# VectorE's order in the attention stage set anew: keys, logits, division and second maximum; logits in another bank; one product left out

## What is computed

```
# cross attention: 16 heads of 8 features, 77 keys per sequence
q = (query @ Wq.T + bq).reshape(B, T, H, HD)      # query = layernorm(x)
k = (key_value @ Wk.T + bk) ...; v = (key_value @ Wv.T + bv) ...
attn = softmax(einsum('bhtd,bhnd->bhtn', q, k) * scale)
x = x + einsum('bhtn,bhnd->bhtd', attn, v) @ Wo.T + bo
# routing, on xf = layernorm(x)
logits = xf @ gate_w.T; probs = softmax(logits)
top_p, top_i = top_k(probs, 2); w = top_p / (sum(top_p) + 1e-09)
rank = cumsum(one_hot(top_i), axis=0) - 1         # place of a token in its expert's list
keep = rank < capacity                            # capacity = 1280
```

## Time and profile before

| | |
|---|---|
| time, median of 3 runs | 1022.3 us (1021.0 to 1023.09) |
| the profiled execution: time | 1019.92 us |
| its span, first to last instruction | 1017.9 us |
| mean granted clock of TensorE | 0.958 of full |
| busy: TensorE, weight loads | 896.1 us, 631.8 us |
| busy: VectorE, ScalarE, GpSimd | 589.0, 468.8, 515.3 us |
| largest groups on TensorE in the middle stage | scores (line 1223) 100.7 us, turned scores (1240) 86.1, weighing (1260) 69.7 |

### The profile page before, as it was taken

The page is one execution under the profiler, slowest core; times in us unless marked ns, Lnnn a source line. Parts: engine busy times, 40 slices in busy tenths (PEclk is TensorE's granted clock), DMA queues, the critical chain, the costliest instruction groups (busy, mean ns, idle before and its releaser), DMA issues.

```text
span 1017.9 us, 26993 instructions
## 1 busy us (share of the span) xinstructions
PE 896.1 (88%) x9394; PEld 631.8 (62%) x9394; DVE 589.0 (58%) x1890; ACT 468.8 (46%) x721; POOL 515.3 (51%) x715
## 2 busy tenths in 40 slices
PE   3699999999999999999999999998349999999960
PEld 1577777776666666666666666666226767667650
DVE  5677777777556676667666766765402222344436
ACT  1256566566445555455555555545123434334320
POOL 4334444454422255555555555555626666666670
PEclk9799999999999999999999999999669999999995
DMA  4369500000000000000000001000021333245408
GB/s 124 104 239 339 191 0 0 0 1 1 7 8 8 8 30 23 29 21 19 12 16 14 15 15 29 9 10 11 16 84 51 102 89 108 80 138 166 147 25 330
DMA packets 49912, 66.68 MB, mean 66 GB/s; under 512 B 12662, under 2 KB 27813, under 8 KB 49824
## 3 DMA queue, kind: packets, MB, share of 16 engines
q1 hardware_dynamic: 38448, 52.14, 15.9%
q0 software_dynamic: 9216, 8.42, 2.8%
q10 hardware_dynamic: 2160, 4.86, 1.2%
HBM read 33.83 MB, written 42.09 MB: 75 GB/s over the span
## 4 chain that ended last, share of the span: by engine, by line
PE 57%; DVE 9%; issue 6%; POOL 2%; DMA 2%; ACT 1%; DVEq 1%; POOLq 0%; SPq 0%; ACTq 0%
PE psum L1677 13%; PE psum L1223 7%; PE psum L1689 7%; PE psum L1260 5%; PE psum L1240 4%; DVE Kb L911 2%; PE psum L1671 2%; PE psum L1273 2%; PE psum L1282 2%; PE psum L1210 2%; DVE Y L1603 2%; PE psum L1226 1%; PE psum L1268 1%; PE psum L594 1%; PE psum L1294 1%
## 5 line engine op out<-in xcount | busy, mean ns | idle before, releaser
L1571 POOL DMA_INDIRECT expert_out<-yo,token x160 | 156.2, 976 | 89.2 <-issue 70.8
L1135 ACT ACTIVATE PT<-psum,key_bias 77x2048 f32<-77x2048 f32 x64 | 125.7, 1964 | 131.1 <-PE psum L1243 131.0
L819 POOL DMA_INDIRECT dispatched<-z,idx x128 | 129.0, 1008 | 84.8 <-issue 42.4
L1614 DVE TENSOR_TENSOR h<-psum,act_g 128x512 f32<-128x512 f32 x80 | 55.3, 692 | 150.7 <-PE psum L1677 150.7
L894 DVE TENSOR_REDUCE top_score<-psum 128x8 f32<-128x616 f32 x128 | 101.9, 796 | 62.1 <-PE psum L1226 60.1
L1223 PE MATMUL psum<-Kb,qT 32*128 32x308 f32 x512 | 100.7, 469 | 0.0
L1649 ACT ACTIVATE act_g<-psum 128x512 f32<-128x512 f32 x80 | 47.8, 597 | 89.2 <-PE psum L1677 89.2
L1240 PE MATMUL psum<-qT,Kb 32*77 32x128 f32 x2048 | 86.1, 283 | 0.0
L1689 PE MATMUL psum<-down,h 128*128 128x128 f32 x640 | 78.1, 275 | 0.8 <-DVE h L1614 0.8
L1677 PE MATMUL psum<-xT,gate 128*128 128x512 f32 (+1 forms) x192 | 77.1, 532 | 0.8 <-ACT xT L1634 0.8
L1689 PEld LDWEIGHTS psum<-down,h 128*128 128x128 f32 x640 | 74.7, 192 | 2.1 <-DVE h L1614 1.7
(11 more groups left out here) (163 smaller groups left out, 1726.6 us busy)
## 6 DMA issues: line engine op xcount, KB each, us to landing
dispatched<-zeros SPq DMA_DIRECT2D x40, 258.0 KB, 2.8
xin<-dispatched SPq DMA_DIRECT2D x40, 258.0 KB, 4.2
expert_out<-zeros SPq DMA_DIRECT2D x32, 256.0 KB, 2.0
X<-in_x SPq DMA_DIRECT2D x16, 256.0 KB, 2.7
yb<-expert_out SPq DMA_DIRECT2D x16, 256.0 KB, 4.0
Y<-expert_out SPq DMA_DIRECT2D x7, 512.0 KB, 8.1
out<-Y ACTq DMA_DIRECT2D x7, 512.0 KB, 6.7
expert_out<-yo,token POOLq DMA_INDIRECT x160, 2.2
```

The costliest lines, as they stand in the source:

```text
L819: pool.indirect_dma_start(xg, bass.IndirectOffsetOnAxis(ap=idx[par][:, t, k:k + 1], axis=0), z4[par][:, t, :], None, bounds_check=ROWS - 1 ...
L1135: nc.scalar.activation(PT[j % 2][:], T.rearrange("p a c -> p (a c)"), ACT.Exp, bias=key_bias[:, bass.ds(b, 1)]).then_inc(s["PT_ready"], 1)
L1571: pool.indirect_dma_start(yt[slot], bass.IndirectOffsetOnAxis(ap=token[i][:, t:t + 1], axis=0), yo[i][:, t, :], None, bounds_check=P * B - ...
```

## The change

- `logits_down` now reads `gate_ps` in bank 0, beside the scores' columns (320 on), instead of in `misc`. It waits for the second half of the scores of batch 4(g + 2) + 2, of the quarter that it stands in (S_ps), instead of for the keys' product. `gate` waits for the first maximum of that quarter (top_ready).
- VectorE, quarter 0: `keys_out` stands right after the first maximum, then `logits_down`, then `normalise`, then the second maximum. Before: logits, second maximum, keys, division.
- VectorE: `ln_stats` and `ln_moments` with n = 3 move from quarter 0 of group g - 2 to quarter 3 of group g - 3, on either side of the steps 13 and 14.
- VectorE: routing steps 3 to 5 move ahead of `add_out`, and steps 6 to 8 from quarter 2 to the end of quarter 1.
- TensorE: the product of `wq` and `z3T` ahead of the turn of `o` is gone, with the waits on `dl_ready`.
- The hardware loop covers groups 4 to 11 instead of 4 to 13; groups 12 and 13 are written out.

```diff
-        gate_ps = misc[:, 320:320 + G4 * E].rearrange("p (t e) -> p t e", t=G4)
+        gate_ps = banks[0][:, 320:320 + G4 * E].rearrange("p (t e) -> p t e", t=G4)
...
-            with eng.Fori(4, NG - 3, 2) as g:
+            with eng.Fori(4, NG - 5, 2) as g:
...
             def logits_down(g):
-                if group(g + 3):
-                    dve.wait_ge(s["k_ps"], g + 4)
+                if group(g + 2):
+                    dve.wait_ge(s["S_ps"], 4 * (G4 * (g + 2) + 2) + 4)
                 dve.wait_ge(s["gate_ps"], g + 1)
...
                     if j == 0:
-                        if group(g + 2):
-                            ln_stats(g + 2, 3, stat3, xrow)
+                        if isinstance(g, int) and g == 0:
+                            ln_stats(2, 3, stat3, xrow)
+                            ln_moments(2, 3, stat3, mom3)
                         if group(g + 1):
                             queries_out(g + 1, other)
...
                     if j == 0:
-                        if group(g + 2):
-                            ln_moments(g + 2, 3, stat3, mom3)
+                        if group(g + 1):
+                            keys_out(g + 1, other)
                         if group(g - 2):
                             logits_down(g - 2)
+                        if batch(b - 1):
+                            normalise(b - 1, G4 - 1, g - 1)
                     if j == 1:
-                        routed(0, 1, 2)
+                        routed(0, 1, 2, 3, 4, 5)
                         if group(g - 1):
                             add_out(g - 1)
                     if j == 2:
-                        routed(6, 7, 8, 9)
+                        routed(9)
                     if j == 3:
+                        if group(g + 3):
+                            ln_stats(g + 3, 3, stat3, xrow)
                         routed(13, 14)
+                        if group(g + 3):
+                            ln_moments(g + 3, 3, stat3, mom3)
 
                     if batch(b + 2):
                         tops(b + 2, j % 2, 1)
-                    if j == 0 and group(g + 1):
-                        keys_out(g + 1, other)
-                    if batch(b - 1):
-                        normalise(b - 1, (j - 1) % G4, g if j else g - 1)
+                    if j > 0 and batch(b - 1):
+                        normalise(b - 1, j - 1, g)
                     if j == 1:
-                        routed(3, 4, 5)
+                        routed(6, 7, 8)
...
             def turn_out(g):
-                nc.tensor.matmul(misc, wq[:], z3T[:], start=True, stop=True)
                 pe.wait_ge(s["o_ready"], G4 * g + G4)
...
             def gate(g):
                 pe.wait_ge(s["z4T_ready"], g + 1)
+                pe.wait_ge(s["top_ready"], 2 * (G4 * (g + 2) + 2) + 1 if group(g + 2) else 2 * NB)
...
                     if j == 1 and group(g - 1):
                         if group(g + 1):
                             pe.wait_ge(s["Kb_ready"], g + 2)
-                        if group(g - 2):
-                            pe.wait_ge(s["dl_ready"], 2 * g - 2)
                         turn_out(g - 1)
```

More of the change, by code:

```diff
@@ L735, in groups @@
                 steps(g, g % 2)
-            with eng.Fori(4, NG - 3, 2) as g:
+            with eng.Fori(4, NG - 5, 2) as g:
                 steps(g, 0)
                 steps(g + 1, 1)
-            for g in range(NG - 2, NG + 3):
+            for g in range(NG - 4, NG + 3):
                 steps(g, g % 2)
```

## The result

The changed kernel took 993.7 us (median; the kernel before 1022.7 us beside it, 1021.0 to 1026.9). The ratio of the two is 0.970, with a 95% interval of 0.966 to 0.974. The forecast was 992.5 us in a range of 986 to 1003. The profiled execution took 991.8 us, its span 990.0, 27.9 less than before. The medians in this document count every execution, the ratios only those within 1.5% of the kernel's fastest: that leaves out one of the four here, which took 1513.0 us at a mean granted clock of 0.61 and of which no trace was taken, so that its cause is open, and in the experiments one of the four with the division last and five of the ten of the unaltered changed kernel.

What follows compares the result with a forecast made beforehand. The prediction took TensorE's nearly unbroken chain of matmuls in the attention stage as the bound. Terms 9.1 + 14.8 + 2.0 + 4.8 + 0.4 - 1.3 = 29.8 us gave 990.1 profiled, 992.5 us as median, range 986 to 1003.

Steps and rivals of the forecast that it cites:

- The chain: Attention stage: TensorE's matmuls run almost without a break, so a microsecond leaving them leaves the kernel 13 or 14 times over.
- the rival in which ScalarE sets the pace: Attention loop: ScalarE paces it, so TensorE would wait elsewhere for what it saves; no change, 1020 to 1024 us; chance 0.04.
- 0.65 (keys): First quarter of a group: TensorE's wait for the keys before the overwritten product goes, 14 x 0.65 = 9.1 us.
- 0.96 (product): First quarter, before the output's turn: removing the overwritten product saves 0.96 us a group, 14.8 us in all.
- 0.37 (`hot`): Before the rank products: routing steps 3 to 8 come earlier, so TensorE's wait for `hot` goes, 13 x 0.37 = 4.8 us.
- 0.15 (qT, 2.0 in 13): First quarter: with statistics moved to the fourth, TensorE's wait for qT goes, 4 times 0.5, 2.0 us in all.
- the 1.3 us given back to ScalarE: ScalarE normalises for the router until 493.69, so exponentials start slightly later than they could: 0.1 x 13 = 1.3 us lost.
- The margins: Slack before TensorE waits: 0.4 us for the first quarter's second maximum, 0.5 for Mx in the first and fourth quarters.
- Both rivals with a late engine: VectorE late at the first quarter's turn, 999.5 us, chance 0.13; GpSimd late with Mx in the fourth, 999 us, chance 0.08.
- The tail: Last 16 scatters, before the experts: the whole shift reaches them, plus some 0.4 us; the last scatter starts near 716.
- The clock, as a rival: TensorE without the overwritten product: its granted clock falls and the kernel gets slower; chance 0.04 together with other causes.

## Why the prediction was right, point by point

- **The chain.** That TensorE's unbroken row of matmuls sets the pace was the ground of the sum, and it stood: of 30 waits none is left, the group went from 27.35 to 25.12 us, and the rival in which ScalarE sets the pace is refuted, since ScalarE's work did not change.
- **The sum.** A group was to lose 0.65 (keys), 0.96 (product), 0.37 (`hot`) and 0.15 (qT, 2.0 in 13), less 0.1. It lost 2.23. The experiments give the product 0.93 and `hot` 0.42; with 0.65 for the keys and 0.15 for qT, which no run singled out, that is 2.15, and 0.08 stay open. So the step on `hot` was sized a little low (0.37 for 0.42), and the 1.3 us given back to ScalarE, taken because it would still be normalising, were not given back: the exponentials follow without a gap, and TensorE never waits for them.
- **The margins.** The second maximum started 6.58 us after the query product against 6.7, and Mx in quarter 3 started at 485.52 and was done 0.8 us ahead of its turn, at 486.81 (0.5 forecast). Doubling the maximum brought waits of 0.25 us on average, so the margin was as thin as stated. Both rivals with a late engine were rightly placed as near and did not come, but for one wait for Mx of 0.45 us, in group 15, and one for the second maximum of 0.32 us, in group 0.
- **The tail and the experts: errors that cancel.** The last scatter was to start near 716 and started at 715.70 (745.96 before), 30.3 us earlier against 29.8 in the sum. The path there was another: at the turn of `o` in quarter 1 of group 15 (666.09 against 697.68) the shift was already 31.6, since each group lost more than counted, and the tail gave 1.3 back instead of adding 0.4. That the two nearly cancel is luck. The rows from group 15 on:

```profile
672.90 0.22 PE L1237 MATMUL psum<-ident_b,Mx 128*128 128x128 bf16 x1 [0.45 <-POOL Mx L795]
...
684.80 1.12 PE L1280 MATMUL psum<-ident,o 128*128 128x128 f32 x4 [0.68 <-DVE o L904]
...
715.70 0.97 POOL L820 DMA_INDIRECT dispatched<-z,idx  x1 [0.30 <-issue]
```

The last turn of `o` took 1.12 us (0.60 at the full clock), and the stretch before the experts ran at 0.72 and 0.54: the clock fell earlier, against the tail's work, than before. Then the span came out only 27.9 us shorter, so 2.4 of the 30.3 were lost in the experts' stage. The fall of the clock after the wait at 852.40, seen above, has 2.2 of them. The sum had no term for it. So the profiled execution took 991.8 us instead of the 990.1 of the sum, and the median lay 1.9 us above it instead of 2.4.
- **The clock, as a rival.** It was priced at "one group in four" and given 0.04 with other causes. In groups 2 to 14 of the changed kernel's profiled execution it did not come. The run with the maximum three times, and the kernel before without its product, show that the mechanism is real where a gap of 0.9 to 1.2 us stands in each group. In the changed kernel real matmuls fill the product's place, so there is no such gap. The Trainium skill, "TensorE: Matmul & The Clock Gate", section "Part 1: The HAM clock gate (the 'warmup' mystery)", says that the engine is throttled by default and that activity lifts it; the traces agree, since each fall named here follows idle time of TensorE. In these traces gaps well under a microsecond were enough for some of the falls (0.39 us once), and far longer ones than those did not always bring one (2.34 us at 882.51).
- **What was missed.** On a chip of the other kind the changed kernel is slower than before. Nothing in the trace of the kernel before, taken on a chip without the stops, hinted at it, and the range of 986 to 1003 says nothing about such a chip. That the measurement fell on the other kind is luck.

## What to carry to other kernels

When one engine runs without a break, count its gaps and its useless instructions per loop, and then read, engine by engine, what stands next in time: here the keys and the quotient had to come earlier before the product could go, and the product alone brought a third of its length at most (0.25 to 0.35 of 0.96 us). Leave margins at the places where the busy engine waits, for a gap can cost several times its own length once the clock falls. And time a tight order on more than one chip, with the unchanged kernel beside it, before calling it better: the same edit was worth -3.0% on one and +1.7% on another.

## What the runs showed of the hardware

- The granted clock of TensorE can fall after a short gap in a stream that is busy otherwise. After 0.90 us of idle time it went to 0.50 for about 6 us and cost some 3 us (group 2 of the run with the maximum three times), and it did so after 7 of that run's 14 gaps of 0.9 to 1.7 us in groups 0 to 13. After 0.39 us it fell once in 13 like gaps (group 2 of the run with the routing back: 26.93 us instead of 25.43); the other 12 left it at 1.00.
- Two chips ran the kernel before in 1076 us instead of 1022 to 1026. On these, what waits for TensorE's matmuls in quarter 1 was released some 3 us late, once in nearly every group, in all eight traces (five different kernels). They have the numerators' wait on a remote event 11 to 13 times each. The cause is open.
